# Expert up and gate bias: from a TensorE product per tile to a VectorE sum from a replicated table

## The reference

```
gate = xf @ router_W[j] + router_b[j];  ids = top_k(gate + gate_bias[j], 2)
weights = softmax(gate over the two chosen experts)
h = xf @ exp_Wup[e] + exp_bup[e]                        # 6 experts, width 256
h = silu(h @ exp_Wg[e] + exp_bg[e]) * h
combined = sum over the two experts of weight * (h @ exp_Wdown[e] + exp_bdown[e])
share_out = (the same form with the shared weights, two halves, summed)
y = xf + combined + share_out;  xf = y * rsqrt(mean(y*y) + eps) * norm_w[j]
```

## Time and profile before

| engine | busy us | share of the span |
|---|---|---|
| PE (matmul) | 2691.3 | 92% |
| PEld (weight load) | 2235.4 | 77% |
| DVE | 1954.0 | 67% |
| ACT | 1722.0 | 59% |
| POOL | 1942.0 | 67% |

### The profile page before, as it was taken

One profiled execution on the slowest core, in us unless ns is written; L12 is line 12 of the kernel. 1 busy time (PEld: TensorE's weight loads), 2 busy tenths in 40 slices (PEclk: granted clock), 3 DMA queues, 4 the chain that ended last, 5 costly groups with the idle time before them and its releaser, 6 DMA issues. The chain is left out here.

```text
span 2911.1 us, 47628 instructions
## 1 busy us (share of the span) xinstructions
PE 2691.3 (92%) x13656; PEld 2235.4 (77%) x13656; DVE 1954.0 (67%) x4383; ACT 1722.0 (59%) x4016; POOL 1942.0 (67%) x1739
## 2 busy tenths in 40 slices
PE   5899999999999589999999999969998999979995
PEld 4588888888888458888888888868886887768884
DVE  3777877777785377877787777535564455664466
ACT  2477777777778347777777777833323443224442
POOL 2598988998999459898899899942262321463235
PEclk9799999999999779999999999989998999879997
DMA  3011111111111101111111111144342443223553
GB/s 74 14 36 31 36 36 32 36 36 38 30 32 39 47 14 36 32 35 36 39 28 36 39 28 32 39 147 139 111 142 98 142 149 95 80 102 127 178 174 116
DMA packets 158331, 197.14 MB, mean 68 GB/s; under 512 B 57964, under 2 KB 122482, under 8 KB 157048
## 3 DMA queue, kind: packets, MB, share of 16 engines
q1 hardware_dynamic: 144760, 160.17, 18.8%
q0 software_dynamic: 12288, 33.57, 3.6%
q10 hardware_dynamic: 1024, 0.26, 0.0%
HBM read 119.95 MB, written 88.65 MB: 72 GB/s over the span
## 5 line engine op out<-in xcount | busy, mean ns | idle before, releaser
L372 POOL TENSOR_TENSOR pl<-pr,ph 128x512 fp32r<-128x512 f32 (+3 forms) x1184 | 1376.4, 1186 | 184.4 <-ACT ph L626 164.0
L623 ACT ACTIVATE pr<-ps 128x512 f32<-128x512 f32 (+3 forms) x1280 | 690.3, 539 | 401.9 <-DVE ps L751 187.6
L800 DVE TENSOR_REDUCE part<-ps 128x1 f32<-128x512 f32 (+3 forms) x1152 | 703.3, 617 | 128.7 <-PE ps L460 112.8
L626 ACT ACTIVATE ph<-ps 128x512 fp32r<-128x512 f32 (+3 forms) x1280 | 689.3, 539 | 0.0
L460 PE MATMUL ps<-k_hi,q_parts 128*128 128x512 f32 (+3 forms) x1280 | 497.1, 391 | 36.9 <-DVE part L800 32.4
L474 PE MATMUL ps<-q_parts,k_hi 128*128 128x512 f32 (+3 forms) x1280 | 483.6, 378 | 0.3
L494 PE MATMUL ps<-ph,v_hi 128*128 128x512 f32 (+3 forms) x1280 | 471.6, 368 | 2.2 <-POOL pl L372 1.8
L475 PE MATMUL ps<-q_row,k_lo 65*128 65x512 f32 (+3 forms) x1280 | 472.3, 369 | 0.0
L495 PE MATMUL ps<-ph,v_lo 128*128 128x512 f32 (+3 forms) x1280 | 468.4, 366 | 0.0
L496 PE MATMUL ps<-pl,v_hi 128*128 128x512 f32 (+3 forms) x1280 | 465.6, 364 | 0.0
L460 PEld LDWEIGHTS ps<-k_hi,q_parts 128*128 128x128 f32 x1280 | 246.0, 193 | 137.9 <-DVE part L800 60.1
(11 more groups left out here) (215 smaller groups left out, 3876.8 us busy)
## 6 DMA issues: line engine op xcount, KB each, us to landing
x_slots<-zero_rows SPq DMA_DIRECT2D x64, 296.0 KB, 4.0
work<-x_slots SPq DMA_DIRECT2D x148, 128.0 KB, 2.5
e_slots<-work SPq DMA_DIRECT2D x148, 128.0 KB, 1.7
rec<-recip_rows SPq DMA_DIRECT2D x128, 128.0 KB, 3.5
y_latent<-y_sums SPq DMA_DIRECT2D x128, 128.0 KB, 3.2
yg<-y_latent SPq DMA_DIRECT2D x32, 512.0 KB, 5.1
acc_shared<-accw SPq DMA_DIRECT2D x14, 512.0 KB, 3.7
accr<-acc_shared SPq DMA_DIRECT2D x12, 512.0 KB, 4.4
```

Of the source, the lines that this page charges most:

```text
L372: eng.tensor_tensor(pl[:, s % RING, 0:w], pr[:, s % RING, 0:w], f32(ph[:, s % RING, 0:w]), ALU.subtract).then_inc(sem, 1)
L623: act.activation(pr[:, s % RING, 0:w], src, ACT.Exp).then_inc(S["probs"], 1)
L626: act.activation(ph[:, s % RING, 0:w], src, ACT.Exp).then_inc(S["probs_hi"], 1)
L800: ins = dve.tensor_reduce(dst, src[:, 0:w], AX.X, ALU.max)
```

## The change

- The up and gate bias is no longer a product. The table `exp_biases` (6 x 512, complete once `bias_sum` is 4) is stored to DRAM at r = 4. At the start of each tile stage SP reads it back into all 128 partitions (`load_bias`: four experts, 1 MB; two experts, 0.5 MB) into `tile_b`, which lies over `xt` and `gg`, for this purpose made one tensor `xt_gg`.
- `tile_add(t)` on VectorE adds the expert's row to the finished sums in PSUM. It reads the expert's number with a `value_load` of its own. `tile_silu(t)` waits for it (`t_add`) instead of for TensorE (`t_up`).
- VectorE's order in iteration t is now add(t), g_lo(t-1), gated(t), then the rest.
- `shared_down(7)` moves ahead of the first tile's transpose.

```diff
+                def load_bias(c):
+                    blk = (8, LATE[0])[c]
+                    if c == 0:
+                        sp.wait_ge(S["bias_kept"], DMA)
+                    else:
+                        sp.wait_ge(S["routed"], 16)
+                    sp.wait_ge(S["up"], 4 * blk)
+                    sp.dma_start(tile_b[:, 0:4, :], bias_dram[0:4, :].unsqueeze(0).broadcast_to([P, 4, 2 * I])).then_inc(S["bias_in0"], DMA)
+                    sp.wait_ge(S["down"], 2 * blk)
+                    sp.dma_start(tile_b[:, 4:E, :], bias_dram[4:E, :].unsqueeze(0).broadcast_to([P, E - 4, 2 * I])).then_inc(S["bias_in1"], DMA)
...
+                    if r == 4:
+                        sp.wait_ge(S["bias_sum"], 4)
+                        sp.dma_start(bias_dram, W["exp_biases"][:, 0:2 * I]).then_inc(S["bias_kept"], DMA)
...
                     for t in range(first, first + 3):
                         load_tile(t)
+                    load_bias(c)
                     if c == 0:
                         store_acc(7)
...
                     out = ps[:, TU + t % 2, :]
-                    tile_bias(out, t, slice(0, 2 * I))
                     terms = [(x, b, dt) for x, b in ((0, 0), (0, 1), (1, 0)) for dt in range(DT)]
                     for n, (x, b, dt) in enumerate(terms):
                         mm = pe.matmul(out, tx[:, t % 2, x, dt, :], wu[:, b, bass.ds(expert[t], 1), dt, :],
-                                       start=False, stop=n == len(terms) - 1)
+                                       start=n == 0, stop=n == len(terms) - 1)
...
                     first, end = 2 * TILES * c, 2 * TILES * (c + 1)
+                    if c == 0:
+                        shared_down(7)
                     turn_tile(first)
                     turn_tile(first + 1)
                     for t in range(first, end + 2):
                         if t < end:
                             tile_up(t)
-                        if t == 0:
-                            shared_down(7)
...
                 def tile_silu(t):
-                    act.wait_ge(S["t_up"], t + 1)
+                    act.wait_ge(S["t_add"], t + 1)
...
+                def tile_add(t):
+                    g, s = t // TILES, t % TILES
+                    if t % (2 * TILES) == 0:
+                        dve.wait_ge(S["tiles"], g + 1)
+                        for k in range(2):
+                            dve.wait_ge(S[f"bias_in{k}"], DMA * (t // (2 * TILES) + 1))
+                    elif s == 0:
+                        dve.wait_ge(S["tiles"], g + 1)
+                    expert = dve.value_load(F["tile_i"][0:1, g % 2, s:s + 1], min_val=0, max_val=E - 1)
+                    dve.wait_ge(S["t_up"], t + 1)
+                    out = ps[:, TU + t % 2, :]
+                    dve.tensor_tensor(out, out, tile_b[:, bass.ds(expert, 1), :].rearrange("p a n -> p (a n)"), ALU.add).then_inc(S["t_add"], 1)
...
                     for t in range(first, end + 1):
                         if t < end:
+                            tile_add(t)
+                        if first <= t - 1:
+                            tile_glo(t - 1)
+                        if t < end:
                             tile_gated(t)
                         if t == 0:
                             take_shared(7)
-                        if first <= t - 1:
-                            tile_glo(t - 1)
                         if t + 2 < end:
                             tile_lo(t + 2)
```

More of the change, by code:

```diff
@@ L912, with build_tokens @@
 LATE = (14, 15)
-def build_tokens(nc, W, F, w, x_v, out_v, y_v, x_slots, e_slots, acc_dram, x1_dram):
+def build_tokens(nc, W, F, w, x_v, out_v, y_v, x_slots, e_slots, acc_dram, x1_dram, bias_dram):
     with ExitStack() as ctx:
@@ L927, in build_tokens @@
                  "scattered0", "scattered1", "scattered2", "scattered3",
-                 "up", "silu", "gated", "g_sum", "g_hi", "g_lo", "down", "acc", "acc_stored",
+                 "bias_kept", "bias_in0", "bias_in1", "t_add", "up", "silu", "gated", "g_sum", "g_hi", "g_lo", "down", "acc", "acc_stored",
                  "xg_in0", "xg_in1", "xg_in2", "xg_in3",
@@ L958, in build_tokens @@
         xt, gg, accw, accr = F["xt"], F["gg"], F["accw"], F["accr"]
+        tile_b = f32(F["xt_gg"][:, :, :, :]).rearrange("p k a n -> p (k a) n")[:, 0:E, :]
         sup, sdn, wu = W["sup"], W["sdn"], W["wu"]
@@ L2233, in build_mixture @@
     acc_dram = nc.dram_tensor("acc_shared", [2 * NBLK, P, TPB, D], F32).ap()
+    bias_dram = nc.dram_tensor("bias_kept", [E, 2 * I], F32).ap()
     x1_dram = nc.dram_tensor("x1_kept", [NBLK, P, TPB, D], F32).ap()
@@ L2251, in build_mixture @@
         W["count"], W["steps"], W["own"] = sb("count", [P, TILES]), sb("steps", [P, JT]), sb("own", [P, 1])
-        F = {"yy": sb("yy", [P, 2, 4, BLK], F32R), "xt": sb("xt", [P, 2, DT, BLK], F32R), "gg": sb("gg", [P, 2, 2, BLK], F32R),
+        F = {"yy": sb("yy", [P, 2, 4, BLK], F32R), "xt_gg": sb("xt_gg", [P, 2, 4, BLK], F32R),
              "pick": sb("pick", [P, 2, TILES], F32R),
@@ L2269, in build_mixture @@
              "own_parts": sb("own_parts", [P, E])}
+        F["xt"], F["gg"] = (F["xt_gg"][:, k].rearrange("p (a t) n -> p a t n", a=2) for k in range(2))
         early = F["accr"][:, :, :, :].rearrange("p r j d -> p (r j d)")
@@ L2274, in build_mixture @@
         y_v = y_dram.rearrange("b q p h n -> (b q) p h n")
-        build_tokens(nc, W, F, w, x_v, out_v, y_v, x_slots, e_slots, acc_dram, x1_dram)
+        build_tokens(nc, W, F, w, x_v, out_v, y_v, x_slots, e_slots, acc_dram, x1_dram, bias_dram)
 def build(nc, w, out):
```

## The result

The changed kernel takes 2970.17 us (median of four runs, 2967.71 to 2973.66), the kernel before 2909.09 in the same comparison: 1.0215 times as long, 95% interval [1.0195, 1.0236]. The forecast was 2976. The profiled executions have spans of 2911.1 and 2967.4 us, 56 apart where the sum said 66; the medians are 61 apart (the profiled execution of the kernel before, 2912.84, was slower than its four timed ones). There is one trace for each kernel, and stretches outside the tile stages wander: hybrid and hybrid_square, which run the same code up to silu of tile 5, differ there by 3.7 us. Sixteen executions of the kernel before ranged from 2899 to 2918. So differences of 3 to 4 us in such stretches, and of some 10 us in a whole span, are not evidence.

What follows compares the result with a forecast made beforehand. TensorE bound the tiles at 2.90 us; after the change the ring would. Plain -3, units 32, normalizes 18, starts 8 + 15, less 4: +66 on 2912.8, 2979; as a median 2976, range 2925 to 3050 (8 in 10).

Steps and rivals of the forecast that it cites:

- the sum: Whole kernel: plain tiles -3, units 32, normalizes 18, starts 8 + 15, less 4, together +66 us.
- The ring: Tile stages: add, silu, g_hi, g_lo, gated, lo, next add in in-order queues; 2.70 us, with register load 2.87 a plain tile.
- The product's worth: TensorE's 512-column bias product, 0.31 us a tile or 0.23 between products; its removal leaves 2.60 to 2.67 us a tile.
- rival 4: Tile stages: TensorE stays the bound, so 34 to 46 us go, total 2870; chance 0.05.
- The load starts when lo is released: VectorE's queue: the register load does not run ahead but starts when lo's wait ends, at 1.97 us after the add starts.
- The price 0.9: VectorE, each tile: 0.9 us for the register load, register steps and the next add's own start.
- unit tiles: Tiles that also add a gathered unit: next add at 4.14 us, 1.24 over 2.90; 26 such tiles, 32.2 us.
- Unit and normalize: Three tiles a stage: 5.21 us in the first, 2.3 x 3 = 6.9; second adds 1.4, 3.7 x 3 = 11.1.
- Routing: Tiles 0 to 4 of a stage: 5.0 us and four of 4.83, together 9.8 us over five tiles of 2.90.
- the first start: First stage: add at 2226.7, silu of tile 5 at 2252.9 against 2245.2 before, 7.7 us later.
- The table's wait: Second stage start: first add waits 8 us for the table, until 2626.5; with routing, silu comes 15.3 us later.
- Hidden waits: Around 2760 to 2830: slower tiles hide waits for rows from DRAM, less 4 us.

Runs made afterwards that it cites:

- hybrid: Kernel before, but in tiles 8 to 40 of each stage the add with early register load and silu and gated last replaces the product: 2892.43 us, ratio 0.9936.
- hybrid_square: hybrid with ScalarE's square of a gathered unit one tile later: 2889.21 us, ratio to the kernel before 0.9921.
- ring_cut: load_early with silu last before the square on ScalarE, and units and routing right after the add, gated last on VectorE: 2902.77 us, ratio to before 0.9976.
- fixed_row: Changed kernel without VectorE's register load, every tile adding the biases of expert 0: 2938.13 us, ratio to the kernel before 1.0108.
- no_bias: Changed kernel with neither add nor bias product, silu waiting for TensorE: 2890.24 us, ratio to the kernel before 0.9952.
- load_early: Changed kernel with VectorE's register load for the next tile moved right behind the add: 2943.33 us, ratio to the kernel before 1.0125.

## Why the prediction was right, step by step

- **The ring** is shown twice: its steps stand in the trace at the predicted offsets, and taking it out by order alone (ring_cut) brings the plain tiles to TensorE's 2.66. Its floor of 2.70 is in fixed_row. The plain gain of 0.03 a tile was 2.3 us over the two plain stretches (74 tiles). Most of their tiles take 2.83 to 2.88; 2.87 is the average.
- **The product's worth**, 0.23 to 0.31 where TensorE is the bound: 0.22 measured in no_bias (8.1 us over 37 tiles). 34 to 46 us over all tiles, as rival 4 had it, was too much even with no add at all: no_bias gains 14 us by its ratio (8 to 20 by the interval; 26 by span, from the slow trace of before), because of the circle through the square, which I had not seen. In the earlier trace rows I wrote that today no circle closes through the two vector engines; true of plain tiles, wrong of those with a unit.
- **The load starts when lo is released**: shown by its start at 2294.33, 0.05 behind hi's end. The price 0.9 was 0.87 on average in plain tiles (most often 0.85), but 0.74 where a unit goes ahead: most unit tiles are 3.97 to 4.07 instead of 4.14. All 26 average 4.03, which is 0.11 x 26 = 3 us of the overestimate. By the Trainium skill, "Perfetto Trace Analysis", section "DVE / Act Engine Instruction", the load would have gone ahead during the wait; the trace disagrees. What the load does overlap is the execution of an instruction whose wait is over. The 600 ns floor of the Trainium skill, "DMA: Bandwidth & Descriptors", section "Latency and other measured facts", does not hold here either: the median is 0.41 us.
- **Unit and normalize**: 5.20 in the first stage (predicted 5.21), 6.53 in the second (6.6).
- **Routing**: predicted 5.0 and four of 4.83, 24.3 in all; the second stage took 21.9 from silu 74 to 79. The small steps were oversized, by 2.4 us there. At the first start everything up to silu 5 cost 4.7 where I had 7.7: the first add came at 2225.5 and not 2226.7 (shared_down had begun at 2216.2, not 2217.6), and the five tiles with take_shared took 23.6 and not 25.5. Here one step was wrong. I let the table's last part (4.4) hide behind the 5.3 from the first transpose to the end of up. That way took only 3.2 (2220.5 to 2223.7), since the tile's rows were there already; the table landed in 3.7 and came last, and a wait and a load of 1.1 followed. That the time of the add fits so well is luck.
- **The table's wait**: first add 2652.1, 8.8 behind the first tile load, where I had 9.7 (2616.81 to 2626.5). The two parts landed in 5.0 and 6.2 us, not 8. Routing and table together with the shared blocks between, 15.1 (predicted 15.3): that is luck too, the sizes were off with errors of opposite sign. 3.8 of it lies in "between" beyond the table's 2.0, a stretch that wanders from 177.7 to 185.8 over the kernels; its cause I did not follow.
- **Hidden waits**: the unit stretches of before were 91.1 and 97.4 us where 31 x 2.90 is 89.9, so 8.7 us of waits stood in them, and the slower tiles hide nearly all. I had subtracted 4.
- **The sum**: 56 of span against 66. The mechanism was right; unit tiles (3), hidden waits (4 to 5) and the first start (3) make up the difference, the last of them no larger than what two traces of the same code differ by.

Not tried: splitting the normalize over several tiles, which is what is left for the unit stretches, and what the slow register loads come from.

## What to carry to other kernels

Moving work from a full engine to one that is idle a third of the time did not pay here while a circle closed through the orders of the two vector engines, and hardly paid over the whole kernel once it was cut (0.9976): write down the ring add, silu, split, split, add with its offsets before believing in idle shares, and put first in each queue what depends on the previous tile and last what depends on this one. A circle of nearly the bound's length is invisible until the bound falls. Where such a move gains in one kind of tile and costs in another, do it in the one kind only.

## What the runs showed of the hardware that I had not expected

- A register load from SBUF on VectorE takes 0.30 us in the shortest case, but 0.41 as the median in this order; load to dependent add mostly 0.74 to 0.88 with three register steps (0.19 one of them, 0.06 the add's own).
- Some register loads take twice the time, on TensorE's queue too, with no load on VectorE at all (fixed_row, 0.66 at 2258.1, and again at 2272.2, 2286.3, 2300.3 and 2314.3, 14.1 apart). I first took this for a collision of the two engines' loads in load_early, where at 2291.5 VectorE's took 0.70 and TensorE's 0.60; fixed_row refutes that as the only cause.
- A 128x512 add of PSUM and SBUF into PSUM takes 0.70 us, 0.02 more than with its output in SBUF.
